# A state-space layer whose C is spread by transfers through memory, with two banks for projections and a VectorE add ahead of the sums

## What is computed

```
x, z = split(u @ W_in.T + b_in);  dbc = x @ W_x.T + b_x
delta = softplus(dbc[:8] @ W_dt.T + b_dt);  B = dbc[8:24];  C = dbc[24:40];  A = -exp(A_log)
h[d,n] = h[d,n] * exp(delta[d] * A[d,n]) + x[d] * delta[d] * B[n]      # for each position t
y[d] = sum over n of h[d,n] * C[n];   y = (y + x * D) * silu(z);   out = y @ W_out.T + b_out
x = layernorm(u + out)
```

## Time and profile before

| | us |
|---|---|
| median of 3 runs (5440.34 to 5486.16) | 5484.78 |
| the profiled execution, its own time | 5422.67 |
| its span, first to last instruction | 5420.9 |
| first scan of the stage starts / last starts | 47.3 / 1183.1 |

### The profile page before, as it was taken

How to read it: one execution, slowest core, us unless ns; L and a number is a source line. 1 busy time by engine, 2 the same in 40 slices (tenths; PEclk the granted TensorE clock), 3 DMA queues, 4 the chain that set the end, 5 groups by cost and what they waited for, 6 DMA issues and landing times. The chain is left out here.

```text
span 5420.9 us, 115532 instructions
## 1 busy us (share of the span) xinstructions
PE 4463.6 (82%) x45878; PEld 2859.8 (53%) x45878; DVE 2708.3 (50%) x6222; ACT 2237.0 (41%) x4042; POOL 1969.7 (36%) x1710
## 2 busy tenths in 40 slices
PE   7888888877888855799997555888878869999999
PEld 3444444444555533455554344555545547777776
DVE  4667766765665523334443444666634433333333
ACT  5555555533445422244443222555445533333332
POOL 5666666655667633111111322666601100000000
PEclk7888988988999977778798777999979979999999
DMA  1000000000000000000000000000000000000000
GB/s 46 5 5 5 2 5 5 2 11 1 2 2 2 2 11 0 12 3 4 3 4 8 0 3 4 1 0 0 1 10 5 6 34 5 4 4 6 4 4 6
DMA packets 20856, 32.04 MB, mean 6 GB/s; under 512 B 6032, under 2 KB 15248, under 8 KB 19984
## 3 DMA queue, kind: packets, MB, share of 16 engines
q1 hardware_dynamic: 20496, 26.78, 1.6%
HBM read 22.58 MB, written 4.19 MB: 5 GB/s over the span
## 5 line engine op out<-in xcount | busy, mean ns | idle before, releaser
L502 DVE TENSOR_TENSOR_SCAN XC<-ssm_dA,ssm_db 128x2048 f32<-128x2048 f32 x128 | 565.4, 4417 | 233.4 <-PE ssm_db L336 233.4
L594 POOL TENSOR_TENSOR XC<-XC,XB 128x1536 f32<-128x1536 f32 x128 | 510.7, 3990 | 408.9 <-PE ssm_y L351 234.5
L2380 PEld LDWEIGHTS experts_out<-experts_wt,experts_hid 128*128 128x128 f32 x4096 | 477.3, 192 | 60.8 <-issue 60.8
L351 PE MATMUL ssm_y<-XC,ssm_wt 128*128 128x512 f32 x1024 | 494.4, 628 | 0.9 <-POOL XC L594 0.9
L2380 PE MATMUL experts_out<-experts_wt,experts_hid 128*128 128x128 f32 x4096 | 477.8, 275 | 0.0
L2446 ACT ACTIVATE experts_hid<-experts_hid,experts_bias 128x512 f32<-128x512 f32 x384 | 263.8, 687 | 505.8 <-PE experts_hid L2400 505.8
L2400 PE MATMUL experts_hid<-experts_zT,experts_wt 128*128 128x512 f32 x1024 | 465.4, 597 | 0.0
L2511 DVE SCALAR_TENSOR_TENSOR experts_acc<-experts_out,experts_gate,experts_acc 128x128 f32<-128x128 f32 x512 | 144.2, 344 | 495.7 <-PE experts_out L2380 487.3
L124 POOL TENSOR_SCALAR experts_rstd<-experts_mv 128x4 f32<-128x4 f32 x32 | 7.3, 228 | 945.9 <-DVE experts_mv L119 945.9
L1104 POOL TENSOR_TENSOR self_pm<-self_pT,self_wt 128x512 f32<-128x512 f32 x256 | 320.7, 1291 | 68.8 <-ACT self_pT L895 68.8
L351 PEld LDWEIGHTS ssm_y<-XC,ssm_wt 128*128 128x128 f32 x1024 | 211.5, 207 | 234.9 <-issue 232.9
(11 more groups left out here) (412 smaller groups left out, 9474.3 us busy)
## 6 DMA issues: line engine op xcount, KB each, us to landing
experts_wt<-in_w_experts SPq DMA_DIRECT2D x1, 4256.0 KB, 13.2
ssm_xT<-in_xT SPq DMA_DIRECT2D x16, 256.0 KB, 2.7
out<-experts_res SPq DMA_DIRECT2D x16, 256.0 KB, 2.3
self_wt<-in_w_self SPq DMA_DIRECT2D x1, 1412.0 KB, 6.1
mlp_wt<-in_w_mlp SPq DMA_DIRECT2D x1, 1347.0 KB, 5.6
cross_ctx_t<-in_ctx SPq DMA_DIRECT2D x16, 77.0 KB
narrow_cT<-in_ctxT SPq DMA_DIRECT2D x16, 77.0 KB, 2.2
cross_wt<-in_w_cross SPq DMA_DIRECT2D x1, 1220.0 KB, 6.9
```

Of the source, the lines that this page charges most:

```text
L351: mm = pe.matmul(yp[half][:, :].rearrange("p (b t) -> p b t", b=GROUP), ident, of_state(states(32, at), k), start=False, stop=(nq == 3 and ...
L502: dve.tensor_tensor_scan(states(0, p).rearrange("p m t -> p (m t)"), dA[:, p % 2, :], db[:, :], 0.0, ALU.mult, ALU.add).then_inc(h_ready, 1)
L594: pool.tensor_tensor(states(32, p).rearrange("p (b k) t -> p b k t", k=4)[:, :, 0:3, :], states(0, p).rearrange("p (b k) t -> p b k t", k= ...
L2380: mm = pe.matmul(yp[k % 2][:, b * C:(b + 1) * C], hid[:, k % 2, j, b * T:(b + 1) * T], w2[:, (k * NF + j) * C:(k * NF + j + 1) * C], start ...
```

## The change

1. **C through memory.** The splitting, the spreading matmuls and ScalarE's copies go, with the tiles `rest`, `parts`, `spread` and bank `cp`. SyncE writes the 16 rows of C to a buffer in device memory (`c_put`, 32 KB), waits for its landing, and reads them back four states at a time into XB, each row onto all 128 partitions (`c_get`, 1024 KB). The rows of w_x are laid out anew, so that C stands in rows 0 to 15 of `dbc` and dt in rows 32 to 39; the bank's copy reorders the columns.
2. **Two banks for the projections.** `pj` becomes a list of two banks; matmul j of a pair goes to bank j and waits for the copy that last read that bank.
3. **An add on VectorE.** In step p, right behind its multiplication, VectorE adds products 0 and 1 of step p-1, both GpSimd's; TensorE then sums three tiles in place of four and waits for this add (`paired`) instead of GpSimd's product.

```diff
+            def c_put(g, slot):
+                sp.wait_ge(proj_read, g * N_ACT + 3)
+                sp.dma_start(cdram[slot], dbc[0:N, :]).then_inc(c_out, 16)
+                sp.wait_ge(c_out, g * 16 + 16)
+
+            def c_get(g, slot, nq):
+                if needed(2 * (4 * g + nq) - 2):
+                    sp.wait_ge(hC_pool, 2 * (4 * g + nq) - 2)
+                    sp.wait_ge(hC_dve, 2 * (4 * g + nq) - 2)
+                sp.dma_start(XB[:, 32 + 16 * (nq % 2):48 + 16 * (nq % 2), :],
+                             bcast(cdram[slot].rearrange("n (b t) -> (n b) t", b=GROUP)[16 * nq:16 * nq + 16, :], 0, P))\
+                    .then_inc(c_in[nq % 2], 16)
+
+            def step(g, slot):
+                for nq in (1, 2, 3):
+                    c_get(g, slot, nq)
+                if more(g):
+                    c_put(g + 1, 1 - slot)
+                    c_get(g + 1, 1 - slot, 0)
...
                 if p == 5:
                     for j in range(2):
-                        pe.wait_ge(proj_read, at + 5 + j)
-                        if needed(g - 1):
+                        pe.wait_ge(proj_read, at + 4 + j)
+                        if j == 0 and needed(g - 1):
                             pe.wait_ge(r_ready, g - 1)
-                        pe.matmul(pj[:, :], w_in[:, (2 + j) * P:(3 + j) * P], xT[:, slot, :]).then_inc(proj_mm, 1)
+                        pe.matmul(pj[j][:, :], w_in[:, (2 + j) * P:(3 + j) * P], xT[:, slot, :]).then_inc(proj_mm, 1)
...
                         pe.wait_ge(hC_dve, u + 1)
-                        pe.wait_ge(hC_pool, u + 1)
-                        for k in range(4):
+                        pe.wait_ge(paired, u + 1)
+                        for k in (0, 2, 3):
...
-                        dve.wait_ge(C_ready, g * N + 4 * nq + 4)
+                        c_there(dve, g, nq)
                         if needed(u - 1):
                             dve.wait_ge(y_mm, u - 1)
                         dve.tensor_tensor(of_state(states(32, p), 3), of_state(states(0, p), 3), c_wide(nq, 3), ALU.mult)\
                             .then_inc(hC_dve, 1)
+                    if now := lagged(g, p, 1):
+                        u, at, _ = now
+                        if there(g) or p == 0:
+                            dve.wait_ge(hC_pool, u + 1)
+                            dve.tensor_tensor(of_state(states(32, at), 0), of_state(states(32, at), 0),
+                                              of_state(states(32, at), 1), ALU.add).then_inc(paired, 1)
```

More of the change, by code:

```diff
@@ L231, in there, with run @@
             return not (isinstance(g, int) and not 0 <= g < NG)
-        def run(eng, head, ahead, step):
+        def run(eng, head, step, ahead=None):
             for p in range(U):
                 head(0, 0, p)
-            ahead()
+            if ahead:
+                ahead()
             step(0, 0)
@@ L256, in fetch @@
                 sp.dma_start(xT[:, slot, :], env["xT"][:, bass.ds(g * GT, GT)]).then_inc(xT_in[slot], 16)
-            with sp.Fori(2, NG - 1, 2) as g:
-                fetch(g, 0)
-                fetch(g + 1, 1)
+            def c_put(g, slot):
[15 more added lines that the diff above has]
+                    c_get(g + 1, 1 - slot, 0)
+            c_put(0, 0)
+            c_get(0, 0, 0)
+            step(0, 0)
+            with sp.Fori(1, NG - 2, 2) as g:
+                fetch(g + 1, 0)
+                step(g, 1)
+                fetch(g + 2, 1)
+                step(g + 1, 0)
+            step(NG - 1, 1)
         @block.tensor
@@ L366, in step @@
                         head(g + 1, 1 - slot, p)
-            run(pe, head, ahead, step)
+            run(pe, head, step)
         @block.scalar
@@ L429, in decay @@
                 o.then_inc(dA_ready, 1)
-            def c_copy(g, nq, k):
-                n = g * N + 4 * nq + k
-                act.wait_ge(C_mm, n + 1)
-                last = 2 * (4 * g + nq) - 2
-                if needed(last):
-                    act.wait_ge(hC_pool, last)
-                    act.wait_ge(hC_dve, last)
-                act.activation(c_wide(nq, k).rearrange("p b (c t) -> p b c t", c=4), by_chunk(cp[:, :]), ACT.Copy).then_inc(C_ready, 1)
-            def ahead():
-                decay(0, 0, 0)
-                for k in range(4):
-                    c_copy(0, 0, k)
-            def c_next(g, p, i):
-                nq, k = p // 2 + 1, 2 * (p % 2) + i
-                if nq < 4:
-                    c_copy(g, nq, k)
-                elif more(g):
-                    c_copy(g + 1, 0, k)
             def step(g, slot):
@@ L459, in step @@
                         decay(g + 1, 1 - slot, 0)
-                    c_next(g, p, 0)
                     if more(g):
                         head(g + 1, 1 - slot, p)
-                    c_next(g, p, 1)
-            run(act, head, ahead, step)
+            run(act, head, step, lambda: decay(0, 0, 0))
         @block.vector
@@ L528, in step @@
                         head(g + 1, 1 - slot, p)
-            run(dve, head, lambda: None, step)
+            run(dve, head, step)
         @block.gpsimd
@@ L607, in step @@
                         head(g + 1, 1 - slot, p)
-            run(pool, head, lambda: None, step)
+            run(pool, head, step)
 def wide_attention_phase(nc, env, name, wd, w, kind):
@@ L2600, in decoder_kernel @@
         env["xT"] = dram["xT"]
+        env["c_rows"] = dram["c_rows"]
         env["ctx"] = dram["ctx"].rearrange("b s c -> s b c")
```

143 lines of the change are left out of this document (50 added, 93 removed).

## The result

The changed kernel takes 5633.41 us (median of 4 runs, 5609.92 to 5643.89) against 5469.92 us for the kernel before (4 runs, 5440.34 to 5486.16): a ratio of 1.0299, 95% interval 1.0237 to 1.0361, so slower by 3.0%. The forecast was 5658 us in a range of 5580 to 5740, slower.

What follows compares the result with a forecast made beforehand. The kernel was taken as a ring of waits, no engine full. For 127 steps 1132.8 + 99 + 3 + 69 + 15 = 1319 us, less 1135.8 = +183; with the start +173, so 5485 + 173 = 5658 us, range 5580 to 5740.

Steps and rivals of the forecast that it cites:

- The port wait (1): VectorE's add waits behind GpSimd's product every step, so no step is under 8.92 us: 1132.8 us for 127 steps; 82%.
- The extras (2): VectorE's other work per group comes on top of the steps: 6.6 us, 99 for 15 groups, 3 for the last.
- Step 5 to 6 (3): TensorE waits for the residual, then makes z and db at 1.2 GHz: 15.6 us, 4.6 more, 15 times 69.
- TensorE elsewhere (4): TensorE's lighter work is worth nothing where scans don't wait for it; late sums cost 15 us, bounds 0 and 100.
- The start (5): Dropped ScalarE copies and GpSimd splitting count only before the first scan: -10 of the 47.3 us.
- The transfers (6): C's four 1024 KB transfers a group land in 5 to 6 us, needed about 22 us later, so hidden.
- The signs: Profile after: add about 3.9 us, scans 8.9 to 9.0 apart, VectorE busy about 500 us more, hardly waiting for TensorE.
- The faster rival: VectorE's add follows its multiplication at once, ahead of GpSimd's product; steps need 5.7 us, TensorE sets many: 5319 us; 12%.

Runs made afterwards that it cites:

- e3: Changed kernel with the add ahead of VectorE's multiplication instead of behind it: 5496.36 us, ratio 1.011.
- e10: Changed kernel without the add, with the z matmuls moved from step 5 to step 7, behind the transposes: 5226.21 us, ratio 0.9616.
- e8: Changed kernel with the add behind VectorE's silu product, residual and statistics, ahead of the normalisation: 5524.53 us, ratio 1.0152.
- e1: Changed kernel without the add, TensorE again summing four tiles; C through memory and both banks stay: 5279.56 us, ratio 0.9701.
- e5: Changed kernel without the add and with one projection bank and its old waits, so C through memory alone: 5418.54 us, ratio 0.9945.
- e13: Changed kernel with GpSimd's product also waiting for VectorE's multiplication of the same step: 5328.83 us, ratio 0.9792.
- e6: Changed kernel with the add moved from VectorE to GpSimd, behind its own product: 5289.57 us, ratio 0.9714.
- e2: Kernel before with the add, its semaphore and the three matmuls alone; C by matmuls and one bank as before: 5681.69 us, ratio 1.0439.
- e4: Changed kernel with four one-input BATCH_NORM_STATS2 in the add's place, same wait and semaphore: 5268.51 us, ratio 0.9732.

## Why the prediction was right, point by point

**The port wait (1)** held in direction, place and size. The add's median is 3.92 us and GpSimd's product 3.94, and the steps without extras take 8.9 us, as summed (19 of the 127; one, before the first add, takes 6.5). One place had GpSimd first, by 0.03 us; there the multiplication took 3.96 us and the add 0.68, and the sum was the same, as written. The weak point was the reason given: I read that GpSimd goes next because it already waits, which e3 narrows to where it has stood there for some 0.3 us.

**The extras (2)** held one by one: four L132 take 1.11 us, L473 2.08, residual and statistics 2.1 (506.91 to 509.03, below).

**Step 5 to 6 (3)** is 14.5 us in the mean for 15.6 forecast, -16 us over 15 groups. VectorE and TensorE there:

```profile
498.03 4.41 DVE L486 TENSOR_TENSOR_SCAN XC<-ssm_dA,ssm_db 128x2048 f32<-128x2048 f32 x1
...
506.91 0.68 DVE L510 TENSOR_TENSOR ssm_r<-ssm_pj,ssm_xr 128x512 f32<-128x512 f32 x1
...
508.65 0.38 DVE L119 BATCH_NORM_AGGREGATE ssm_mv<-ssm_stats 128x2 f32<-128x6 f32 x4 [0.15 <-DVE ssm_stats L115]
512.99 4.42 DVE L486 TENSOR_TENSOR_SCAN XC<-ssm_dA,ssm_db 128x2048 f32<-128x2048 f32 x1 [3.96 <-PE ssm_db L346]
```

```profile
507.74 3.75 PE L325 MATMUL ssm_pj<-ssm_xT,ssm_wt 128*128 128x512 f32 x4 [8.67 <-DVE ssm_r L510]
511.42 1.49 PE L346 MATMUL ssm_db<-XB,ssm_dxT 32*128 32x128 f32 x32
```

The idle TensorE starts at its low clock, 3.75 us for the two matmuls (3.8 forecast; granted clock 0.50 over them), but the clock rises while `db` is made (0.76 over it), 1.49 us where I had 2.09. Also, where the prediction counts 7.5 us from L520's start to db's end today, its rows give 8.15 (458.08 to 466.23), 7.5 from L520's end; the sum did not use it. e10 and e8 confirm the cause from two sides: without the wait ahead of `db`, or with the residual 3.9 us earlier, the step is short.

**TensorE elsewhere (4)** was the term that was mis-sized: 15 us taken, while steps 2-3 and 3-4 together took 38 us more than their terms (0.7 and 1.8 us, 15 times). The bounds, 0 to 100, held it. I had a late sum at 1.2 GHz holding VectorE back by 0.8 us, and left out what goes ahead of the sums: I did not follow who stands behind the add on VectorE. L505 does, and TensorE's first matmul of that half's output, L355, waits for L505 to have read the bank. VectorE, TensorE and two windows of the same place:

```profile
559.94 0.68 DVE L505 TENSOR_TENSOR ssm_yg<-ssm_y,ssm_zs 128x512 f32<-128x512 f32 x1
560.54 4.40 DVE L486 TENSOR_TENSOR_SCAN XC<-ssm_dA,ssm_db 128x2048 f32<-128x2048 f32 x1
567.52 0.69 DVE L492 TENSOR_TENSOR XC<-XC,XB 128x512 f32<-128x512 f32 x1 [2.57 <-PE ssm_y L360]
```

```profile
560.68 2.08 PE L355 MATMUL ssm_y<-ssm_xi,ssm_skip 128*128 128x512 f32 x2 [3.13 <-DVE ssm_yg L505]
562.55 4.83 PE L360 MATMUL ssm_y<-XC,ssm_wt 128*128 128x512 f32 x6
```

```profile
560.00:565.00 5.00, 4.32 (x5) 1.85 (x6) 4.95 (x3) 2.89 (x4) 0.00 (x0) 0.50 0.00 0
565.00:570.00 5.00, 3.48 (x36) 1.66 (x34) 2.48 (x2) 2.53 (x4) 2.45 (x1) 0.82 0.00 0
```

L355 starts with the scan, at 1.2 GHz (granted clock 0.50 from 560 to 565) after an idle 3.13 us, the sums end 2.4 us after the scan, and the multiplication waits 2.57 us for them. It is the clock more than the start: in e1, too, L355 starts beside the scan, but takes 1.12 us in place of 2.08, at 2.4 GHz (granted clock 1.00) behind a busy TensorE. One step earlier in the changed kernel the same lines also met 2.4 GHz (1.00 from 552.0 to 554.7):

```profile
551.05 1.12 PE L355 MATMUL ssm_y<-ssm_xi,ssm_skip 128*128 128x512 f32 x2 [0.20 <-DVE ssm_yg L505]
552.01 2.74 PE L360 MATMUL ssm_y<-XC,ssm_wt 128*128 128x512 f32 x6
```

There the sums end 0.7 us before the scan and the step takes 9.5 us, as forecast; in the five groups where step 2-3 met the low clock it takes 11.7 to 11.9. e8, where L505 stands ahead of the add, has 8.9 us at both steps, 47 us less over 15 groups. That shows the cause: the add is paid twice there, once on VectorE and once through the TensorE work that it keeps waiting.

**The start (5)** is -14.3 us for -10. e5, with one bank, starts its first scan at 38.3, 9 us earlier than before: the C part was right. The second bank gives the rest, which I left out (33.9 in e1, 33.0 here). **The tail**, +5.9 us from the last scan to the stage's end, stood nowhere in my sum.

**The transfers (6)** were hidden, as forecast: no wait of the scan, the multiplication or the product names one. Landing took 4.7 us in the median (4.0 to 7.9 over both kinds), for 5 to 6 estimated:

```profile
XB<-c_rows SPq DMA_DIRECT2D x64, 1024.0 KB, 4.7
```

So 1319 us were forecast for the 127 steps and 1337.6 came: +23 in (4) (38 for 15), -16 in (3), and +12 in what is left, 5 of it in the last group and 7 in steps 4-5 and 7-0. Errors of both signs partly cancel.

**The total.** 5658 us were forecast and 5633 came, 25 less: 10 because the difference between the medians was +163 for +173, and 15 because the kernel before ran that much faster beside the changed one than in the runs shown first. By the profiles the first stage alone grew by 193 us. So that the total came within 25 us is in part luck: 20 us too little for the stage, and scatter of the whole runs the other way. The upper end of the range, 5740, leaves out the 46 us of scatter that the text adds; it did not matter here.

**The signs.** VectorE's busy time rose by 418 us over the span (2708 to 3126) for 500 announced: the add's 495, less among others 44 for L132, which no longer stands behind GpSimd's product (59.3 to 15.5 us). VectorE still waits for TensorE, 55 us ahead of the scan and 59 ahead of the multiplication, less than before but more than "hardly".

The faster rival, 12%, needed VectorE's second instruction to go ahead of the product. The chip does that at a hand-over in 8 steps of e3, with GpSimd 0.32 or 0.33 us behind the first; the changed kernel, with GpSimd some 0.04 us behind, never did it. e13 reaches the rival's order by a wait in the program, with GpSimd 0.82 us behind or more, and 5329 us where the rival was priced at 5319; that the two numbers are so near is partly chance, since its step 4-5 takes 11.7 us for 8.0 in the rival's list.

## What to carry to other kernels

Before putting a two-input VectorE instruction behind another one, look for a GpSimd instruction that starts at the same event: here the second of the two is as long as GpSimd's whole instruction, and no wait shows it, only a duration of 3.9 us for work of 0.7. Then order by who is waited for: what TensorE needs next goes ahead of the add, and one more wait that lets GpSimd start behind VectorE's pair can be worth more (300 us here) than the work moved. A quarter of TensorE's sums, moved to GpSimd, brought nothing (e6). A second bank brought 124 us of stage without the add; with the add, C through memory and the bank brought only 66 together (e2 against the changed kernel).

## What the runs showed of the hardware that I had not expected

- The hand-over of the shared access is not simply to the one that waits. With VectorE's two instructions back to back, GpSimd got the turn between them when it had started up to 0.30 us after the first, and both happened from 0.32 to 0.35 us (e3). From 0.82 us on the second was already running (e13). What decides inside that band stays open, and no run has a start between 0.35 and 0.82 us.
- The normalisation L132, one tensor and two columns of scalars from SBUF, also runs behind GpSimd's product: 1118 ns in the mean in e1, 335 in e3, where the product has ended by then. BATCH_NORM_STATS2 does not (278 ns in e4).
- TensorE's granted clock rose within a block of work: `db` took 1.49 us right behind 3.75 us of matmuls at 1.2 GHz (granted clock 0.50, then 0.76), against 2.09 in the kernel before and 1.17 at 2.4 GHz.
